# Gated linear attention beside an MLP: the recurrence's running products, block products and carry one round earlier, the split of keys and queries right behind the fourth states, the queries' negation later

## The chip, the core and the metric

The program runs on one core of a Trainium2 chip. The metric is the device time of one execution in microseconds (us). The kernel computes four transformer layers one after the other; the change touches only one function, `gla`, and in it only the written-out order of the work.

## What is computed

Four layers, each an attention-like half and a feed-forward half, over 8 batches of 512 tokens with 128 channels. The change lies where the kernel runs two of these halves together: the feed-forward half of layer 1 (8 experts of 128 by 512) and the attention half of layer 2, a gated linear attention with 8 heads of 32 complex channels:

```python
u = silu(x @ W_in.T + b_in)
q, k, v, a = complex(u @ W_qkva.T + b_qkva)          # (b, 512, 8, 32) each
mag2 = a.real * a.real + a.imag * a.imag
a = a * (rsqrt(mag2) * sigmoid(log(mag2)))           # |a| is the decay, a/|a| a turn of phase
kv = einsum('blhd,blhe->blhde', k, v)
_, h = associative_scan(lambda c1, c2: (c1[0]*c2[0], c2[0]*c1[1] + c2[1]), (a, kv), axis=1)
y = einsum('blhd,blhde->blhe', q, h)
x = x + ga * (silu(y @ W_y.T + b_y) @ W_out.T + b_out)
```

The kernel takes the phases out of the scan: with U the running product of a/|a| along the tokens, q and k are multiplied ("turned") by U or its conjugate, and the scan is left with real decays. It then works by blocks of 32 tokens (and 8 and 16 within them).

## The kernel before

**Stages.** `gla` runs 19 stages, numbered n = 0 to 18. Each of the engines PE (TensorE), DVE (VectorE), ACT (ScalarE) and POOL (GpSimd) walks all stages in its own program, in order, and waits on counting semaphores. A stage mixes work of several batches: `sg` names the group of four heads whose scan is computed (stages 2 to 17), `tg` the group whose q, k and decays are prepared for the next stage (1 to 16), `mg` the group whose projections are made for the stage after that (0 to 15; norm and input projection are made with group 0), `ob` a batch whose output projection is made (even stages from 4 to 18), `half` one half of the experts of a batch (stages 0 to 13). So stages 2 to 13 carry everything; 14 to 17 have no expert matmuls; an even stage from 4 on has the output steps, an odd one has not.

**Order.** Within a stage the order is the tuple `ORDER`, a list of (what, which). Every engine takes from it the steps for which it has a function, so that one list sets the order on all four. A step that an engine's function ignores costs it nothing.

**The steps that matter here.** Four rounds i = 0 to 3 of 128 tokens each: `scores (i, 0..3)` (192 small matmuls, L1279), `gains i` (64 small matmuls, L1295), both on PE; `sums i` and `states i` on DVE (L1530 to L1536; L1545, L1548), which wait for them; `outputs (i, 0..4)` on PE (L1315, L1321), which wait for DVE's sums and states of that round. PE's `scores (i+1, 0)` waits for DVE's `states i`.

Preparation of group `tg`, nearly all on DVE: `decays` (L1580 to L1594), `run0` and `run1` (running products within 16 tokens, 7 and 8 steps of three small operations, L1614 to L1617), `values` (L1601, waits for PE's L1335), `blocks` (products over blocks, L1619 to L1639), `carry` (U, L1645 to L1648, then ACT negates one plane of it, L1492), `turned` (six operations of 128x1024, L1654 to L1657, the first of which waits for ACT's negation), `split` (Q, six operations, L1665; then the keys `ks`, L1667, and queries `qs`, L1669). `split` waits for the last scores of the stage, since these read the old Q and K. POOL's part of `split` (K, six operations, L1245) waits for `kh` of `turned` and for the last scores. ACT's part negates one plane of each Q (L1496); PE's `scores (0, 0)` of the next stage waits for ACT's Q and POOL's K, PE's `keys` (L1260) for DVE's `ks`:

```python
elif i: ...                                             # scores (i, 0) for i > 0 waits for DVE's s and h
else:
    e.wait_ge(act.steps, act.at(was("qneg")))
    e.wait_ge(pool.steps, pool.at(was("K")))
```

`make units` is a chain: DVE (L1566), ACT (L1463 to L1468), POOL (L1229 to L1235, four operations), and DVE's `logs` (L1569). On POOL it stands ahead of `split`.

Output of batch `ob`: `out hidden` (PE, L1373), `out gate` (DVE L1674 and L1676, then three on ACT: L1422, L1424, L1502), `out gated` (DVE, L1679), `out last` (PE L1377, ACT L1505, DVE L1683). PE's `keys` of the next stage waits for ACT's L1505.

**The dense matmuls.** 16 pairs `up i` and `down i - 4` per stage. `up i` (PE, L1388) writes one PSUM bank, and waits until ACT's Relu (L1510) has read `up i - 1` out of it:

```python
if i:
    e.wait_ge(act.steps, act.at(now(f"r{i - 1}")))
e.matmul(P[2], fc[:, n % 2, ts(f, C)], hs[:, n % 2], ...)    # up i
```

ACT follows each Relu by a Square (L1512), for which `down i` (PE, L1402) waits. `up 4 n` also waits for DVE's `root n` (L1689). In an even stage `down 12` to `down 15` are left to the next stage, where they stand as `down -4` to `down -1`; in an odd stage they come at its end. SP loads the experts' weights into two slots each, every load behind the `up` or `down` that used the slot last.

Of the kernel before, what the change touches and what calls it, by code (L numbers as in the profile page):

```python
# [1077 lines left out]
def gla(k, a, gate_rows, h_rows):  # L1078

    nc = k.nc  # L1080
    with ExitStack() as s:
# [44 lines left out]
        def half_of(ap, i, later_half):  # L1126

            if i == 0:
# [10 lines left out]
                 ("scores", (1, 2)), ("outputs", (0, 2)), ("scores", (1, 3)), ("outputs", (0, 3)), ("outputs", (0, 4)), ("turn", "values"), ("gains", 1),  # L1139
                 ("root", 1), ("up", 4), ("down", 0), ("sums", 1), ("states", 1), ("make", "hidden"), ("up", 5), ("down", 1), ("make", "gate"),  # L1140

                 ("scores", (2, 0)), ("outputs", (1, 0)), ("up", 6), ("turn", "run1"), ("scores", (2, 1)), ("outputs", (1, 1)), ("down", 2),
                 ("scores", (2, 2)), ("outputs", (1, 2)), ("make", "gated"), ("scores", (2, 3)), ("outputs", (1, 3)), ("outputs", (1, 4)), ("gains", 2),
                 ("root", 2), ("up", 7), ("down", 3), ("sums", 2), ("states", 2), ("make", "decay"), ("up", 8), ("down", 4), ("turn", "blocks"),

                 ("scores", (3, 0)), ("outputs", (2, 0)), ("make", "query"), ("scores", (3, 1)), ("outputs", (2, 1)), ("scores", (3, 2)),
                 ("outputs", (2, 2)), ("make", "key"), ("scores", (3, 3)), ("outputs", (2, 3)), ("outputs", (2, 4)), ("gains", 3), ("turn", "carry"),
                 ("up", 9), ("down", 5), ("make", "units"), ("sums", 3), ("states", 3), ("root", 3), ("up", 10), ("down", 6), ("turn", "turned"),

                 ("outputs", (3, 0)), ("up", 11), ("outputs", (3, 1)), ("outputs", (3, 2)), ("down", 7), ("outputs", (3, 3)), ("outputs", (3, 4)),  # L1150
                 ("out", "hidden"), ("make", "logs"), ("up", 12), ("down", 8), ("out", "gate"), ("up", 13), ("down", 9), ("turn", "split"), ("up", 14),
                 ("down", 10), ("up", 15), ("down", 11), ("out", "gated"), ("out", "last"), ("down", 12), ("down", 13), ("down", 14), ("down", 15),
                 ("residual", 0))
# [18 lines left out]
        def units():  # L1172
# [17 lines left out]
            with nc.Block() as block:  # L1190
# [217 lines left out]
                def _(e):  # L1408
# [61 lines left out]
                    def turn(what):  # L1470
# [22 lines left out]
                        elif what == "split":  # L1493
# [1098 lines left out]
def build(nc, a, counts, upto=99, first=0):  # L2592
    k = Kernel(nc, counts)
    k.dram = a
    with k.stack:
# [22 lines left out]
        if first <= 3 <= upto:  # L2618
            with ExitStack() as s:
                load(k, a, "gla", s)  # L2620
                gla(k, a, gate_rows, h_rows)
# [123 lines left out]
```

## Time and profile before

| what | value |
|---|---|
| three runs | 4273.81, 4292.37, 4297.87 us; median 4292.37 |
| profiled execution | 4287.15 us, its span 4285.4 us |
| mean granted TensorE clock of that execution | 0.859 of full speed |
| busy share of the span | PE 86%, DVE 54%, ACT 36%, POOL 18% |
| stages 2 to 13 | 947.5 to 2039.3 us, 88 to 96 us each |
| stages 14 to 16 | 2039.3 to 2278.0 us, 82.6, 76.3 and 79.9 us |

The span runs from the first to the last instruction; the profiled execution's own time has 1.75 us more around it. Stages are told apart by PE's `keys` (L1260), which begins each from stage 2 on: 947.5, 1035.6, 1125.0, 1216.9, 1309.0, 1400.6, 1493.4, 1584.3, 1674.6, 1765.6, 1855.3, 1943.2, 2039.3, 2121.8, 2198.2 and 2278.0 us. Stage 7, from 1400.6 to 1493.4 us, is the one that is read closely below.

### The profile page before, as it was taken

To read this page: it belongs to the slowest core of one execution; us is meant where nothing else is said; L and a number is where in the kernel's file an instruction comes from. 1 tells how busy PE (TensorE), PEld (TensorE's weight loads), DVE (VectorE), ACT (ScalarE), POOL (GpSimd) and SP (SyncE) were. 2 spreads that over 40 slices of the span, in tenths; PEclk is the share of its full clock that TensorE was granted. 3 is DMA by queue.
4 is the path that set the end of the run, shared out by engine and by line. 5 is a ranking of instruction groups with operands and counts; after the bars stand their busy time and mean duration, and the time that the engine had idled before them with its cause. 6 is when DMAs were issued, how large, how long until landed. Compare 5 with 4: busy or idle time off the path is not lost. (4 is left out here: it accounts for less than half of the span.)

```text
span 4285.4 us, 124546 instructions
## 1 busy us (share of the span) xinstructions
PE 3686.3 (86%) x55640; PEld 2276.7 (53%) x55640; DVE 2300.0 (54%) x5899; ACT 1558.3 (36%) x2877; POOL 761.2 (18%) x724
## 2 busy tenths in 40 slices
PE   3877776689898888998876987999999999999986
PEld 2336664235554455554554433666666666666672
DVE  3757775267667666676672112444444444444445
ACT  2653333363344443444210433333333333333323
POOL 1212221011112111122110001222222222222210
PEclk9886667798888888988655998999999999999967
DMA  2000000221111111110000000000000000000000
GB/s 83 0 0 1 1 1 1 75 62 37 41 33 41 44 33 39 39 42 27 3 3 17 0 21 40 2 3 2 2 2 2 2 2 3 2 2 2 2 3 22
DMA packets 37030, 79.22 MB, mean 18 GB/s; under 512 B 7568, under 2 KB 11025, under 8 KB 35345
## 3 DMA queue, kind: packets, MB, share of 16 engines
q1 hardware_dynamic: 36496, 71.25, 5.1%
q8 instruction: 440, 7.21, 0.7%
q14 instruction: 94, 0.76, 0.1%
HBM read 66.91 MB, written 4.33 MB: 17 GB/s over the span
## 5 line engine op out<-in xcount | busy, mean ns | idle before, releaser
L2129 PE MATMUL ps<-d_hp,d_w_qk 128*128 128x512 f32 x1024 | 545.8, 629 | 2.7 <-DVE d_hp L2386 2.7
L1388 PE MATMUL ps<-g_hs,g_fc 128*128 128x512 f32 x448 | 289.8, 733 | 82.0 <-ACT g_hidden L1510 75.9
L1510 ACT ACTIVATE g_hidden<-ps 128x512 f32<-128x512 f32 x224 | 133.1, 594 | 377.5 <-PE ps L1388 377.5
L2207 POOL TENSOR_TENSOR d_sq<-d_QK 128x512 f32<-128x512 f32 x128 | 133.0, 1039 | 759.5 <-ACT d_QK L2249 754.1
L1402 PE MATMUL ps<-g_hidden,g_proj 128*128 128x512 f32 x448 | 263.6, 685 | 0.0
L1279 PEld LDWEIGHTS ps<-g_Q,g_K 32*32 32x32 f32 x12288 | 193.9, 113 | 130.1 <-issue 46.6
L1279 PE MATMUL ps<-g_Q,g_K 32*32 32x32 f32 (+1 forms) x12288 | 224.9, 218 | 28.1 <-DVE g_H L1548 12.0
L1229 POOL TENSOR_TENSOR g_tmp<-g_rs 128x512 f32<-128x512 f32 x16 | 26.7, 1667 | 1029.9 <-ACT g_rs L1468 1029.9
L2227 ACT ACTIVATE d_F<-ps 128x128 f32<-128x128 f32 x256 | 70.8, 276 | 381.0 <-PE ps L2043 379.9
L2129 PEld LDWEIGHTS ps<-d_hp,d_w_qk 128*128 128x128 f32 x1024 | 162.5, 190 | 81.9 <-issue 63.4
L1388 PEld LDWEIGHTS ps<-g_hs,g_fc 128*128 128x128 f32 x448 | 82.4, 217 | 191.5 <-ACT g_hidden L1510 144.6
L2185 POOL TENSOR_TENSOR d_M<-d_A,w_joins 128x128 f32<-128x128 f32 (+1 forms) x128 | 114.7, 916 | 385.6 <-ACT d_A L2221 385.6
L2352 DVE TENSOR_TENSOR d_r<-d_r,ps 32x128 f32<-32x128 f32 x192 | 55.0, 286 | 216.5 <-PE ps L2137 121.7
L2086 PEld LDWEIGHTS ps<-d_r,d_Y 32*32 32x32 f32 x2048 | 86.8, 110 | 153.1 <-issue 38.0
L1295 PE MATMUL ps<-g_V,g_KT 32*32 32x64 f32 x4096 | 144.0, 268 | 25.4 <-issue 5.8
L1402 PEld LDWEIGHTS ps<-g_hidden,g_proj 128*128 128x128 f32 x448 | 97.7, 223 | 123.6 <-issue 106.4
L794 PE MATMUL ps<-att_kg,att_qx 32*128 32x96 f32 x1024 | 121.7, 354 | 41.9 <-DVE att_qx L708 27.3
L2036 PE MATMUL ps<-d_QK 128*128 128x128 f32 x1024 | 157.5, 300 | 0.0
L2355 DVE COPY d_W<-ps 32x128 f32<-32x128 f32 x256 | 71.5, 279 | 157.2 <-PE ps L2086 156.1
L2221 ACT ACTIVATE d_A<-d_A 32x128 f32<-32x128 f32 x256 | 78.6, 307 | 210.9 <-DVE d_A L2313 206.3
L2036 PEld LDWEIGHTS ps<-d_QK 128*128 128x128 f32 x1024 | 132.7, 202 | 33.7 <-issue 30.0
L2180 POOL TENSOR_TENSOR d_D<-d_D,w_upto 128x512 f32<-128x512 f32 x64 | 81.0, 1265 | 381.5 <-ACT d_D L2217 381.5
(473 smaller groups left out, 8009.2 us busy)
## 6 DMA issues: line engine op xcount, KB each, us to landing
g_hs<-gate_rows SPq DMA_DIRECT2D x56, 256.0 KB, 3.5
g_fc<-in_c_fc_dram SPq DMA_DIRECT2D x56, 256.0 KB, 3.9
g_proj<-in_c_proj_dram SPq DMA_DIRECT2D x56, 256.0 KB, 2.8
d_QK<-in_conv_qk_dram SPq DMA_DIRECT2D x2, 2048.0 KB, 6.8
X<-in_x_dram SPq DMA_DIRECT2D x1, 2048.0 KB, 11.0
w_c_fc<-in_c_fc_dram SPq DMA_DIRECT2D x1, 2048.0 KB, 7.8
w_c_proj<-in_c_proj_dram SPq DMA_DIRECT2D x1, 2048.0 KB, 12.2
ex_root<-gate_rows SPq DMA_DIRECT2D x1, 2048.0 KB, 15.0
```

The source lines that it names most:

```text
L794: ins = e.matmul(scored[:, g, b], qx[ts(g, 32), q, 4 * u + b, :, :].rearrange("p h q -> p (h q)"), kg[ts(g, 32), q, 4 * u + b, :], start=T ...
L1279: ins = e.matmul(later(scored, n_), keys_, queries(n_, planes, r_, 4 * i + j), start=(turn_ == 0 and part == 0 and n_ != 1), stop=(part == 1),
L1295: ins = e.matmul(P[1][ts(h4, 32), 256 + j * 64:320 + j * 64], KT[rows, (KR, KI)[part], i, ts(h4, 32)], V[rows, i, 4 * c["sg"] + h4, (slice ...
L1388: e.matmul(P[2], fc[:, n % 2, ts(f, C)], hs[:, n % 2], start=True, stop=True).then_inc(pe.steps, pe.did(now(f"u{i}")))
L1402: e.matmul(P[3], proj[:, n % 2, f, :], r[:, (16 * c["half"] + i) % 5], start=(c["half"] == 0 and i == 0), stop=(c["half"] == 1 and i == 15 ...
L1510: e.activation(r[:, slot], P[2], ACT.Relu).then_inc(act.steps, act.did(now(f"r{i}")))
L2036: ins = e.matmul(mk[:, ts(h, C)], QK[:, 1, H, t], QK[:, part - 1, H, t], start=True, stop=True)
L2086: ins = e.matmul(b[rows, 256 + 32 * h:288 + 32 * h], Y[rows, y, h], rv[rows, g, h], start=True, stop=True, tile_position=(32 * j, 32 * j))
L2129: ins = e.matmul(b, w_qk[:, j, c, ts(H, C)], hp_of(u)[:, j:j + T], start=(j == 0), stop=(j == TAPS - 1))
L2180: e.tensor_tensor(D[:, g], D[:, g], k.w["upto3"][:].unsqueeze(1).to_broadcast([C, 4, C]), ALU.mult).then_inc(pool.steps, pool.did(f"d{n}"))
L2185: e.tensor_tensor(M[:, a, levels], A32[:, a].unsqueeze(1).to_broadcast([C, many, 4, 32]), k.w["joins"][:, levels].unsqueeze(2).to_broadcas ...
L2207: e.tensor_tensor(squares(x), qk, qk, ALU.mult).then_inc(pool.steps, pool.did(f"{tag}sq{x}"))
```

## The change

Only `ORDER` and one name change. `run1` moves from round 2 to round 1, ahead of `values`; `blocks` from the end of round 2 to `run1`'s old place; `carry` from round 3 to the end of round 2, between `up 8` and `up 9`; `turned` from behind `states 3` into round 3, ahead of `make units` and `sums 3`; `split` from behind `out gate` and `logs` to right behind `states 3` and `root 3`. ACT's negation of Q, which was ACT's part of `split`, is a step of its own, `negate`, behind `up 14` and `down 10`. `up 9` to `up 12` and `down 5` to `down 8` move forward, `up 9` to `up 11` into rounds 2 and 3; the five `outputs (3, ...)` now stand together; `make logs` moves behind `up 15`.

```diff
-                 ("scores", (1, 2)), ("outputs", (0, 2)), ("scores", (1, 3)), ("outputs", (0, 3)), ("outputs", (0, 4)), ("turn", "values"), ("gains", 1),
-                 ("root", 1), ("up", 4), ("down", 0), ("sums", 1), ("states", 1), ("make", "hidden"), ("up", 5), ("down", 1), ("make", "gate"),
-
-                 ("scores", (2, 0)), ("outputs", (1, 0)), ("up", 6), ("turn", "run1"), ("scores", (2, 1)), ("outputs", (1, 1)), ("down", 2),
+                 ("scores", (1, 2)), ("outputs", (0, 2)), ("scores", (1, 3)), ("outputs", (0, 3)), ("outputs", (0, 4)), ("turn", "run1"), ("turn", "values"),
+                 ("gains", 1), ("root", 1), ("up", 4), ("down", 0), ("sums", 1), ("states", 1), ("make", "hidden"), ("up", 5), ("down", 1), ("make", "gate"),
+
+                 ("scores", (2, 0)), ("outputs", (1, 0)), ("up", 6), ("turn", "blocks"), ("scores", (2, 1)), ("outputs", (1, 1)), ("down", 2),
                  ("scores", (2, 2)), ("outputs", (1, 2)), ("make", "gated"), ("scores", (2, 3)), ("outputs", (1, 3)), ("outputs", (1, 4)), ("gains", 2),
-                 ("root", 2), ("up", 7), ("down", 3), ("sums", 2), ("states", 2), ("make", "decay"), ("up", 8), ("down", 4), ("turn", "blocks"),
-
-                 ("scores", (3, 0)), ("outputs", (2, 0)), ("make", "query"), ("scores", (3, 1)), ("outputs", (2, 1)), ("scores", (3, 2)),
-                 ("outputs", (2, 2)), ("make", "key"), ("scores", (3, 3)), ("outputs", (2, 3)), ("outputs", (2, 4)), ("gains", 3), ("turn", "carry"),
-                 ("up", 9), ("down", 5), ("make", "units"), ("sums", 3), ("states", 3), ("root", 3), ("up", 10), ("down", 6), ("turn", "turned"),
-
-                 ("outputs", (3, 0)), ("up", 11), ("outputs", (3, 1)), ("outputs", (3, 2)), ("down", 7), ("outputs", (3, 3)), ("outputs", (3, 4)),
-                 ("out", "hidden"), ("make", "logs"), ("up", 12), ("down", 8), ("out", "gate"), ("up", 13), ("down", 9), ("turn", "split"), ("up", 14),
-                 ("down", 10), ("up", 15), ("down", 11), ("out", "gated"), ("out", "last"), ("down", 12), ("down", 13), ("down", 14), ("down", 15),
-                 ("residual", 0))
+                 ("root", 2), ("up", 7), ("down", 3), ("sums", 2), ("states", 2), ("make", "decay"), ("up", 8), ("down", 4), ("turn", "carry"), ("up", 9),
+                 ("down", 5),
+
+                 ("scores", (3, 0)), ("outputs", (2, 0)), ("make", "query"), ("scores", (3, 1)), ("outputs", (2, 1)), ("up", 10), ("down", 6),
+                 ("turn", "turned"), ("scores", (3, 2)), ("outputs", (2, 2)), ("make", "key"), ("scores", (3, 3)), ("outputs", (2, 3)), ("outputs", (2, 4)),
+                 ("gains", 3), ("up", 11), ("down", 7), ("make", "units"), ("sums", 3), ("states", 3), ("root", 3), ("turn", "split"), ("up", 12),
+                 ("down", 8), ("outputs", (3, 0)), ("outputs", (3, 1)), ("outputs", (3, 2)), ("outputs", (3, 3)), ("outputs", (3, 4)), ("out", "hidden"),
+                 ("up", 13), ("down", 9), ("out", "gate"), ("up", 14), ("down", 10), ("turn", "negate"), ("up", 15), ("down", 11), ("make", "logs"),
+                 ("out", "gated"), ("out", "last"), ("down", 12), ("down", 13), ("down", 14), ("down", 15), ("residual", 0))
@@ ACT's turn(what)
-                        elif what == "split":
+                        elif what == "negate":
                             for i in range(3):
```

## Rows read from the trace of the kernel before

**Rows 1.** The page's busy time: engine, us, share of the span, instructions
```profile
PE 3686.3 (86%) x55640; PEld 2276.7 (53%) x55640; DVE 2300.0 (54%) x5899; ACT 1558.3 (36%) x2877; POOL 761.2 (18%) x724
```
**Rows 2.** Busy time by stretch: us, PE, PEld, DVE, ACT, POOL, granted clock, DMA share, GB/s
```profile
947.50:2039.30 1091.80, 982.27 (x19624) 556.19 (x19623) 747.19 (x1976) 451.05 (x788) 181.86 (x126) 0.86 0.12 37
2039.30:2278.00 238.70, 180.65 (x4707) 131.34 (x4705) 165.99 (x480) 48.60 (x89) 28.20 (x27) 0.60 0.01 3
...
1400.60:1493.40 92.80, 84.78 (x1637) 47.09 (x1637) 60.20 (x161) 35.84 (x63) 14.91 (x10) 0.83 0.15 45
```
**Rows 3.** PE's waits in stages 2 to 13: total us, times, longest
```profile
PE ps L1388 <- ACT g_hidden L1510: 60.9, 27, 6.7
```
**Rows 4.** Timeline of PE, stage 7: start, us, work, idle before it and releaser
```profile
1462.05 2.19 PE L1295 MATMUL ps<-g_V,g_KT 32*32 32x64 f32 x64
1464.17 2.08 PE L1388 MATMUL ps<-g_hs,g_fc 128*128 128x512 f32 x2
...
1485.61 2.08 PE L1388 MATMUL ps<-g_hs,g_fc 128*128 128x512 f32 x2 [4.24 <-ACT g_hidden L1510]
1487.48 6.08 PE L1402 MATMUL ps<-g_hidden,g_proj 128*128 128x512 f32 x10
1493.40 1.04 PE L1260 MATMUL ps<-w_ident,g_m_ks 128*128 128x128 f32 x8
```
**Rows 5.** Timeline of ACT, stage 7
```profile
1452.48 0.61 ACT L1510 ACTIVATE g_hidden<-ps 128x512 f32<-128x512 f32 x1
...
1484.66 0.42 ACT L1496 ACTIVATE g_Q<-g_Q 128x256 f32<-128x256 f32 x1 [1.32 <-DVE g_Q L1665]
1484.98 0.58 ACT L1510 ACTIVATE g_hidden<-ps 128x512 f32<-128x512 f32 x1
```
**Rows 6.** Timeline of DVE, stage 7
```profile
1424.54 0.69 DVE L1601 TENSOR_TENSOR g_V<-ps,w_b_v 128x512 f32<-128x512 f32 x1 [8.41 <-PE ps L1335]
...
1460.59 0.42 DVE L1530 TENSOR_TENSOR g_S<-ps,w_gla_mask 128x256 f32<-128x256 f32 x1 [4.10 <-PE ps L1279]
...
1464.38 0.29 DVE L1536 TENSOR_TENSOR g_S<-g_S,ps 128x128 f32<-128x128 f32 x1 [2.84 <-PE ps L1295]
...
1466.79 1.22 DVE L1654 TENSOR_TENSOR g_m_qs<-g_raw_qka,g_U 128x1024 f32<-128x1024 f32 x1
...
1472.30 2.28 DVE L1655 TENSOR_TENSOR g_m_ks<-g_raw_qka,g_U 128x1024 f32<-128x1024 f32 x1
...
1477.73 6.89 DVE L1665 TENSOR_TENSOR g_Q<-g_unit_qh,g_F 128x512 f32<-128x512 f32 x6
```
**Rows 7.** Timeline of POOL, stage 7
```profile
1469.18 2.12 POOL L1229 TENSOR_TENSOR g_tmp<-g_rs 128x512 f32<-128x512 f32 x1 [74.22 <-ACT g_rs L1468]
...
1477.23 7.11 POOL L1245 TENSOR_TENSOR g_K<-g_kh,g_E 128x512 f32<-128x512 f32 x6
```
**Rows 8.** Timeline of PE: ends of stages 9 and 8, of stage 1
```profile
1667.19 2.08 PE L1388 MATMUL ps<-g_hs,g_fc 128*128 128x512 f32 x2 [6.72 <-ACT g_hidden L1510]
...
1574.70 1.13 PE L1388 MATMUL ps<-g_hs,g_fc 128*128 128x512 f32 x2 [1.25 <-ACT g_hidden L1510]
...
1578.91 1.53 PE L1388 MATMUL ps<-g_hs,g_fc 128*128 128x512 f32 x2 [2.23 <-ACT g_hidden L1510]
...
940.00 2.07 PE L1388 MATMUL ps<-g_hs,g_fc 128*128 128x512 f32 x2 [8.67 <-ACT g_hidden L1510]
```
**Rows 9.** Timeline of PE, DVE and POOL at the ends of stages 14 to 16
```profile
2118.90 2.07 PE L1377 MATMUL ps<-g_xb,w_W_out 128*128 128x512 f32 x2 [8.32 <-DVE g_xb L1679]
...
2182.32 2.86 PE L1315 MATMUL ps<-g_S,g_V 32*64 32x32 f32 x64 [3.64 <-DVE g_H L1548]
...
2198.17 1.97 PE L1260 MATMUL ps<-w_ident,g_m_ks 128*128 128x128 f32 x8 [10.97 <-DVE g_m_ks L1667]
...
2275.10 2.07 PE L1377 MATMUL ps<-g_xb,w_W_out 128*128 128x512 f32 x2 [7.75 <-DVE g_xb L1679]
...
2182.12 1.22 DVE L1654 TENSOR_TENSOR g_m_qs<-g_raw_qka,g_U 128x1024 f32<-128x1024 f32 x1
...
2189.47 7.16 POOL L1245 TENSOR_TENSOR g_K<-g_kh,g_E 128x512 f32<-128x512 f32 x6 [7.70 <-DVE g_kh L1657]
```

## The prediction

> **What bounds the kernel now.** The page first: PE is busy 86% of the span, DVE 54% [rows 1]. By stretches, stages 2 to 13 hold 982 us of PE work in 1091.8, stages 14 to 16 181 us in 238.7 at a mean clock of 0.60 [rows 2]. So PE is the bound of the first stretch, and what can be won there is PE's idle time, or PE time at the lower clock. PE's waits come next: 60.9 us in 27 waits of `up` (L1388) for ACT's Relu are by far the largest entry [rows 3]. They lie like this: seven long ones of 4.24 to 6.72 us near the end of stages 2, 3, 5, 7, 9, 11, 13 (36.3 us together; the shortest in [rows 4], the longest in [rows 8]); two in each of the even stages 4 to 12, 1.01 to 2.23 us (15.6 us; stage 8's in [rows 8]); and 9.0 us in ten places that the change leaves alone (six of 1.26, four of 0.35 us). Stage 1 has one more, of 8.67 us [rows 8].
>
> Then three timelines of stage 7. ACT's Relu of `up 14` starts at 1484.98, right behind the last negation of Q, which had waited for DVE's Q [rows 5]; `up 15`, which needs the bank that this Relu reads, starts at 1485.61 [rows 4]. DVE makes the six Q from 1477.73 to 1484.6, since `turned`, begun at 1466.79, comes only behind `states 3` and lasts 11 us [rows 6]. So the gap is DVE's lateness passed on by ACT, which stands in its queue before the negation while a Relu that PE wants waits behind it. DVE itself is not full: it sits 8.41 us before `values`, 4.10 before `sums 3`, 2.84 inside it [rows 6].
>
> **The change, part by part, in stage 7.** *`run1` ahead of `values`.* Eight steps at about 0.76 us (1430.5 to 1436.6 before) are 6.0 us, into an idle 8.41 [rows 6]: nothing. In the even stages that idle is shorter by `normed`; `values` comes some 0.5 us late there at most, behind which PE has `gains 1`, `up 4`, `down 0`. Nothing. *`blocks`* (5.2 us) takes the place of the longer `run1`: nothing. *`carry`* (3.6 us) right behind `states 2`: U is ready at about 1450.6. ACT meets its negation behind the Relu of `up 8`, which it does at 1452.48 [rows 5], so ACT does not wait; that needs 2 us of slack and has them. *`turned`* then runs from about 1454.4 (ACT's negation done) with POOL idle, six operations of 1.22 us (the first of them in [rows 6]), 7.4 us, to 1461.8, and `units` 0.7 behind it. Now it stands ahead of `sums 3`. DVE before waited for these until 1460.59 and 1464.38 [rows 6]; with two pairs of `up` and `down` (some 3.8 us) put ahead of them on PE they come at about 1464.5 and 1468.3. Slack 2 us for the first, 5.8 for the one that counts. Nothing, and the rival of the other sign below.
>
> *`root 3` and `up 12`.* `up 12` now follows `down 7`, two pairs earlier in effect. DVE needs `sums`' last step, `states 3` and `root 3`, 2.7 us, from the end of `gains 3`; PE has `up 11` and `down 7` for that, 1.9 us at full clock, 3.8 at half, and behind gains they ran at half (2.08 for two records, 1.0 to 1.1 elsewhere) [rows 4]. A wait of 0 to 1.5 us per stage; I take 0.5, 6 us over twelve.
>
> *`split`* starts at about 1471 instead of 1477.7, but with PE's work ahead of it moved 4 us later this is more than 10 us earlier against PE. Q is done by 1478. `negate` comes on ACT behind `up 14`, about 1482. ACT no longer waits there; its 1.5 us of negations stand ahead of the Relu of `up 15`, for which only `down 15` asks, behind four other `down`. So the long gaps go: -36.3. In even stages DVE's `out gate` now stands behind `split`, which is over by then, and ACT's three operations for it (1.9 us) stand before the Relu of `up 14`; I leave 1.0 of each stage's two gaps: -15.6 + 5 = -10.6.
>
> *POOL.* Its chain starts when ACT has made `units`, behind `up 11` now, behind `up 9` before. Measured from the end of `gains 3` that is the same place. It takes 8 us for units and 7.11 for K [rows 7]: from 1473 to about 1488. PE then wants K for `scores (0, 0)`, one `keys` after its own end: before at 1494.4, now near 1490 or less. Slack 1 to 2 us where there were 10. Nothing, but thin. The Trainium skill, GPSIMD Engine Reference, section Specifications, says that GpSimd shares its SBUF interfaces with VectorE and contends with VectorE instructions that have two SBUF inputs. The trace agrees: `turned` takes 1.22 us an operation without POOL and up to 2.28 beside it [rows 6]. By that rule the new neighbour of `units` (Q instead of `turned`) has two inputs as well, so the price in stages 2 to 13 stays; in stages 14 and 15 it is new (below).
>
> *Stage 1.* It has no recurrence on PE, so DVE is later against PE: `run1` delays `values` and `root 1` by 1.8 us and `turned` before `root 3` delays `up 12` by some 1.3. The 8.67 us gap goes, then PE waits for POOL's K. Bounds 2 and 8.7; I take -5.
>
> *Stages 14 to 16.* No pairs here, DVE close behind PE. Stage 15: DVE had `turned` from 2182.12, POOL K 7.16 us from 2189.47, PE's `keys` only at 2198.17 after 10.97 us [rows 9]. Now `turned` is over by 2175.5, `split` starts at the end of `states 3`, about 2182; POOL beside it lengthens Q to 6.9, `ks` is ready near 2190, K near 2191. PE's `keys` at about 2189.7: -8.5. Stages 14 and 16 end with `out last` waiting for `gated` behind `split` (8.32 and 7.75 us) [rows 9]. Now `gated` waits only for PE's own `out hidden`, `out gate` and ACT: 4.4 us. -3.9 and -3.3. The 3.64 us before `outputs (3, 0)` [rows 9] may lose up to 1.5 if POOL no longer runs beside `states 3`; taken as 0. Together -15.7.
>
> *Clock.* Behind each of eight long gaps the matmuls run at the lower of the two levels: `up 15` took 2.08 us for two records, and `down 11` to `down 15` 6.08 for ten [rows 4], where 12 records at the full rate of 0.43 take 5.2. Over the eight stages 7.0 to 8.1 us (3.2 against 1.9 in the even one) make 19 us. With the gap gone these should go too. Against that: the five `outputs (3, ...)` now stand together, 3 us of small matmuls with no dense one between, and behind such stretches (`scores`, `outputs`, `gains`) PE also fell to the lower level [rows 4]. One such fall per stage would cost 1.7 us, 20 in all. The bounds of this item are -19 and +20; I take -10, half of the gain, since 3 us is shorter than the 4.5 us ahead of 1464. The Trainium skill, TensorE: Matmul & The Clock Gate, section on HAM oscillation, has the rule that idle gaps between bursts throw the clock back to half and that the burst behind pays. The trace agrees behind the gaps. By the rule alone, without the new block, the sum would be 9 us lower.
>
> **SP.** The loads wait for the same `up` and `down`, which come earlier; DMA is busy 12% [rows 2]. Nothing.
>
> **Sum.** -36.3 - 10.6 + 6 - 5 - 15.7 - 10 = -71.6 us. From the profiled execution, 4287.15, that is 4215.5. The median of the three runs is 5.2 above it, and the runs spread over 24 us; I put 2.5 on: 4218.
>
> **The rivals.** (a) *POOL becomes the bound of stages 2 to 13.* K comes at 1488 to 1490, PE asks at 1488 to 1490. For: slack falls from 10 us to under 2, and every us that PE wins is one that POOL does not. Against: in odd stages DVE is through with Q, `ks` and `qs` before K ends, so K should rather be shorter than 7.11 us. If K is 2 us late per stage, 24 us come back: 4242. (b) *The clock takes the gain.* `outputs (3)` in one block costs a fall in every stage and the ends gain nothing: +20 instead of -10, 4248. For: half-speed matmuls behind every small stretch; against: dense pairs now also split `scores (3, ...)`. (c) *`turned` holds up the recurrence: slower.* It stands ahead of `sums 3` in DVE's queue. If it starts late, because ACT reaches U's negation late or runs it behind the evacuations of `query`, then `sums 3`, `states 3`, `root 3` and with them `up 12` and `outputs (3, 0)` wait. It decides once the delay is over the 5.8 us of slack. If all of `turned` fell behind `gains 3`, 7.4 us per stage, 89 us over twelve stand against 72 won: 4304. Against it: ACT gets there at 1453.7 with the operand ready. (d) *Nothing that can be measured.* ACT still waits, for Q at `negate`, or the waits reappear at `up 10` to `up 12`: 4280. That would need Q 4 us later than worked out.
>
> **Chances.** Forecast 0.60, (a) 0.14, (b) 0.13, (c) 0.06, (d) 0.07. What a measurement can tell from no change is about 0.5%, 21 us. (a) and (b) are still faster; so faster 0.87, same 0.07, slower 0.06. Range: below, the full 19 us of clock, no wait at `up 12` and all of stage 1 give about 4188; above, (a) and (b) with a little of both, 4258.
>
> **What would show it.** After: the wait of L1388 for ACT in stages 2 to 13 falls from 60.9 us to 14 to 22, no single one over 2; L1496 no longer ends its idle with DVE's Q; DVE's `turned` operations all at 1.22 us and before `sums 3`; PE waits for L1679 and L1667 at the ends of stages 14 to 16 nearly gone; POOL's K ends within 3 us of `scores (0, 0)`; the mean clock of stages 2 to 13 at 0.86 to 0.88. A stage of 88 us or more, a wait of L1279 for g_K, or a wait of L1388 for g_hs over 1.5 us would make it wrong.

## The result, and the profile after

| | us |
|---|---|
| changed kernel | 4236.88, median of 4 runs (4232.26 to 4240.60) |
| kernel before, beside it | 4295.12, median of 4 (4273.81 to 4309.92) |
| ratio, with its 95% interval | 0.9868 (0.9824 to 0.9911) |
| the changed kernel again, two more times | 4241.44 (5 runs), ratio 0.9886 (0.9866 to 0.9907); 4246.05 (4 runs), 0.9897 (0.9869 to 0.9926) |
| profiled execution | 4237.54, its span 4235.8, mean clock 0.862; before 4287.15, 4285.4, 0.859 |

The change makes the kernel faster by 1.0 to 1.3%, some 50 us (43 to 58 by the medians) where the sum had 72. The measured 4236.88 lies 19 us above the forecast of 4218, inside its range of 4188 to 4258. The profiled executions are 49.6 us apart. From the stage borders of the two traces: up to the keys of stage 2 -3.6 us, stages 2 to 13 -32.4 (1091.8 to 1059.4), stages 14 to 16 -12.5, all that follows -1.1. In stages 2 to 13 PE's idle time fell by 25.8 us (109.5 to 83.7) and its busy time by 6.6.

The page's busy line, and the two stretches that answer to [rows 1] and [rows 2] (us, then PE, PEld, DVE, ACT, POOL, granted clock, DMA share, GB/s):

```profile
PE 3676.4 (87%) x55640; PEld 2273.3 (54%) x55640; DVE 2277.5 (54%) x5899; ACT 1556.2 (37%) x2877; POOL 728.4 (17%) x724
```
```profile
943.90:2003.30 1059.40, 975.69 (x19623) 554.84 (x19622) 721.35 (x1978) 448.26 (x788) 153.53 (x129) 0.87 0.12 38
2003.30:2229.60 226.30, 178.68 (x4708) 130.14 (x4706) 171.11 (x480) 48.52 (x89) 28.48 (x27) 0.60 0.01 3
```

PE's waits in stages 2 to 13 of the changed kernel (us in total, times, longest). Line numbers from `ORDER` on are one lower than before, so L1387 is [rows 3]'s L1388:

```profile
PE ps L1387 <- ACT g_hidden L1509: 19.3, 23, 2.8
PE ps L1320 <- issue: 12.1, 10, 2.6
PE ps L1278 <- issue: 10.2, 12, 2.2
PE ps L1387 <- DVE g_hs L1688: 5.4, 7, 0.8
PE ps L1294 <- issue: 4.4, 8, 0.9
...
PE ps L1278 <- POOL g_K L1244: 2.2, 2, 1.8
```

The entry of 60.9 us is down to 19.3, inside the 14 to 22 of the forecast, though its longest is 2.8 where none was to be over 2. Three others have come or grown: `up 12` waits for DVE's `root 3` (L1688), `scores (0, 0)` for POOL's K (L1244), and the three "issue" entries, in which PE waited for nothing that the profile shows, are 26.7 us where the same view of the kernel before had 10.0, 5.8 and 5.8, or 21.6. In two more traces of the changed kernel the three are 25.6 and 29.2.

Now stage 7 (keys 1385.1 to 1468.0, 82.9 us for 92.8), as four timelines: start, us, work, idle before it and what ended it. PE:

```profile
1454.10 1.12 PE L1387 MATMUL ps<-g_hs,g_fc 128*128 128x512 f32 x2 [0.77 <-DVE g_hs L1688]
...
1462.79 1.12 PE L1387 MATMUL ps<-g_hs,g_fc 128*128 128x512 f32 x2
1463.75 4.45 PE L1401 MATMUL ps<-g_hidden,g_proj 128*128 128x512 f32 x10
...
1469.01 1.21 PE L1278 MATMUL ps<-g_Q,g_K 32*32 32x64 f32 x62
```

`up 15` (1462.79) has no wait ahead of it, and the ten records behind it take 4.45 us where [rows 4] has 6.08: the gap of 4.24 us and the slow matmuls behind it have both gone. ACT and DVE:

```profile
1463.30 1.23 ACT L1495 ACTIVATE g_Q<-g_Q 128x512 f32<-128x512 f32 x3
1464.43 0.57 ACT L1509 ACTIVATE g_hidden<-ps 128x512 f32<-128x512 f32 x1
```
```profile
1437.46 1.23 DVE L1653 TENSOR_TENSOR g_m_qs<-g_raw_qka,g_U 128x1024 f32<-128x1024 f32 x1 [3.75 <-ACT g_U L1491]
...
1447.99 0.42 DVE L1529 TENSOR_TENSOR g_S<-ps,w_gla_mask 128x256 f32<-128x256 f32 x1 [2.53 <-PE ps L1278]
...
1453.36 0.68 DVE L1688 TENSOR_TENSOR g_hs<-g_hx,g_hs 128x512 f32<-128x512 f32 x1
1453.96 4.96 DVE L1664 TENSOR_TENSOR g_Q<-g_unit_qh,g_F 128x512 f32<-128x512 f32 x6
1458.84 3.43 DVE L1666 TENSOR_TENSOR g_m_ks<-g_kh,g_E_lg 128x512 f32<-128x512 f32 x2
```

ACT's three negations run in one piece of 1.23 us, without a wait, behind the Relu and Square of `up 14`. On DVE `turned` begins at 1437.46; between its end and the first `sums 3` the engine still idles for 2.53 us, so it holds nobody up. Q is done 4.4 us before ACT turns to it. POOL:

```profile
1455.40 1.08 POOL L1228 TENSOR_TENSOR g_tmp<-g_rs 128x512 f32<-128x512 f32 x1 [76.02 <-ACT g_rs L1467]
...
1460.00 7.49 POOL L1244 TENSOR_TENSOR g_K<-g_kh,g_E 128x512 f32<-128x512 f32 x6
```

K ends at 1467.49, 1.5 us before `scores (0, 0)` at 1469.01: as thin as forecast, and enough except at the start of stages 2 and 3 (the 2.2 us above). From there on K has 0.6 to 3.4 us to spare at the end of an odd stage, and 3.2 to 8.3 at the end of an even one.

That is not how every stage runs. In stages 2 to 9 of this trace POOL's first operation starts 1.4 us behind DVE's Q, and the two engines' work is as shown. In stages 10 to 13 it starts 1.9 to 2.4 us behind it, and then it is POOL that is held, here in stage 13:

```profile
1985.86 2.63 DVE L1664 TENSOR_TENSOR g_Q<-g_unit_qh,g_F 128x512 f32<-128x512 f32 x6
```
```profile
1988.25 4.14 POOL L1228 TENSOR_TENSOR g_tmp<-g_rs 128x512 f32<-128x512 f32 x1 [80.44 <-ACT g_rs L1467]
```

DVE's whole `split` takes 5.0 us in those four stages, and 11.1 in the other eight.

The even stages kept their length (542.1 us in the six of them for 541.5), the odd ones fell from 550.3 to 517.3. In the even ones PE's waits for ACT's Relu did fall, from 29.0 us to 17.1, but its other idle time rose by some 8 us and its busy time by 4.6, with 146.8 us at the lower clock for 138.8. (Two more traces of the changed kernel have even stages of 545.1 and 546.1 us, with 160.4 and 153.6 us at the lower clock. There is one trace of the kernel before.) One of the waits that are left is at the end of stage 8, DVE first, then PE:

```profile
1542.74 4.95 DVE L1664 TENSOR_TENSOR g_Q<-g_unit_qh,g_F 128x512 f32<-128x512 f32 x6
1547.62 3.42 DVE L1666 TENSOR_TENSOR g_m_ks<-g_kh,g_E_lg 128x512 f32<-128x512 f32 x2
...
1553.78 0.74 DVE L1673 TENSOR_SCALAR g_xb<-ps,w_b_y 128x512 f32<-128x512 f32 x1
```
```profile
1557.93 1.13 PE L1387 MATMUL ps<-g_hs,g_fc 128*128 128x512 f32 x2 [2.76 <-ACT g_hidden L1509]
```

PE's `out hidden` ended at about 1551.6. `out gate` (L1673) reads it only at 1553.78, since `split` stands ahead of it and takes 11.1 us. ACT's three operations for the gate follow that, and the Relu that `up 15` needs follows them: 2.76 us of idle PE. It is the longest such wait. In the other two traces stage 8 has 1.05 and 1.06 us there; `out hidden` ran at the lower clock in these and took 5.40 us instead of 3.70, so the gate was hardly late.

Last, PE at the end of stage 1 and of stages 14 to 16, against [rows 8] and [rows 9]:

```profile
896.78 2.03 PE L1387 MATMUL ps<-g_hs,g_fc 128*128 128x512 f32 x2 [5.34 <-ACT g_F L1484]
```
```profile
2067.50 2.86 PE L1314 MATMUL ps<-g_S,g_V 32*64 32x32 f32 x64 [4.83 <-DVE g_H L1547]
...
2082.77 2.08 PE L1376 MATMUL ps<-g_xb,w_W_out 128*128 128x512 f32 x2 [4.02 <-DVE g_xb L1678]
...
2153.22 1.97 PE L1259 MATMUL ps<-w_ident,g_m_ks 128*128 128x128 f32 x8 [4.14 <-DVE g_m_ks L1666]
...
2226.64 2.08 PE L1376 MATMUL ps<-g_xb,w_W_out 128*128 128x512 f32 x2 [4.01 <-DVE g_xb L1678]
```

The waits for L1679 fell from 8.32 and 7.75 to about 4, the one for the keys of stage 16 from 10.97 to 4.14. Against that `outputs (3, 0)` of stage 14 waits 4.83 us for the states, where it had been 3.64, as in stage 15. The states ran beside POOL's `units` before too; now they also meet the start of its K, and their four 128x32 operations take 3.42 us for 2.22.

### The profile page after: what moved, and what is told of

It reads as the page before. It is cut to its first block and busy times, and to the rows that moved or that the text cites. A ratio compares the mean times of both kernels' runs of the same rounds, so it can differ in the third digit from the quotient of the medians.

```text
span 4235.8 us, 124560 instructions
## 1 busy us (share of the span) xinstructions
PE 3676.4 (87%) x55640; PEld 2273.3 (54%) x55640; DVE 2277.5 (54%) x5899; ACT 1556.2 (37%) x2877; POOL 728.4 (17%) x724
## 5 line engine op out<-in xcount | busy, mean ns | idle before, releaser
L2128 PE MATMUL ps<-d_hp,d_w_qk 128*128 128x512 f32 x1024 | 545.9, 629 | 2.7 <-DVE d_hp L2385 2.7
L1387 PE MATMUL ps<-g_hs,g_fc 128*128 128x512 f32 x448 | 287.6, 728 | 42.2 <-ACT g_hidden L1509 24.2
L1401 PE MATMUL ps<-g_hidden,g_proj 128*128 128x512 f32 x448 | 254.7, 664 | 0.0
L1387 PEld LDWEIGHTS ps<-g_hs,g_fc 128*128 128x128 f32 x448 | 82.9, 216 | 154.3 <-ACT g_hidden L1509 82.0
L2216 ACT ACTIVATE d_D<-d_D 128x512 f32<-128x512 f32 x64 | 40.3, 629 | 294.8 <-DVE d_D L2299 294.8
## 6 DMA issues: line engine op xcount, KB each, us to landing
w_c_proj<-in_c_proj_dram SPq DMA_DIRECT2D x1, 2048.0 KB, 12.5
```

The costliest lines, as they stand in the source:

```text
L1387: e.matmul(P[2], fc[:, n % 2, ts(f, C)], hs[:, n % 2], start=True, stop=True).then_inc(pe.steps, pe.did(now(f"u{i}")))
L1401: e.matmul(P[3], proj[:, n % 2, f, :], r[:, (16 * c["half"] + i) % 5], start=(c["half"] == 0 and i == 0), stop=(c["half"] == 1 and i == 15 ...
L2128: ins = e.matmul(b, w_qk[:, j, c, ts(H, C)], hp_of(u)[:, j:j + T], start=(j == 0), stop=(j == TAPS - 1))
```

## Experiments

Each was timed beside the kernel before; ratios are to that, with the 95% interval. "Idle" is PE's idle time in stages 2 to 13, "low" the time of that stretch in which the granted clock stood at the lower level (before: 109.5 and 303.8 us; changed kernel, three traces: 83.7, 81.0, 84.6 and 279.9, 307.2, 279.9).

**The changed kernel again**, to have its spread beside the variants.

> The changed kernel itself once more, on the chip on which the three below run, so that they can be held against it. Both theories: 0.985 to 0.990 of the kernel before, about 4237 us.

> The changed kernel again, as the one that the three below are held against: ratio 0.985 to 0.991.

4241.44 and 4246.05 us (ratios in the first table). The forecast's shape stands, its size doesn't.

**1. ACT's negation alone.** The kernel before, with only this:

```diff
-                 ("down", 10), ("up", 15), ("down", 11), ...
+                 ("down", 10), ("turn", "negate"), ("up", 15), ("down", 11), ...
@@ ACT's turn(what)
-                        elif what == "split":
+                        elif what == "negate":
```

> The kernel before with one edit: ACT's three negations of Q are a step of their own behind `up 14` and `down 10`, nothing moves on DVE, POOL or PE. Theory A (ACT's place in its queue made the gaps; DVE's lateness by itself costs nothing in stages 2 to 13): the Relu of `up 14` no longer stands behind the negations, so the seven gaps of 4.24 to 6.72 us and the one of 8.67 go, L1388's waits for ACT fall from 60.9 to 15 to 25 us, with some of the clock 40 to 50 us in all, 4245 to 4255 us, ratio 0.988 to 0.991; stages 14 to 16 stay at 82.5, 76.4 and 79.8 us. Theory B (Q must come earlier, the moves on DVE carry the gain): Q is as late as before, the negations now hold the Relu of `up 15`, `down 15` and the end of the stage wait instead; 4285 to 4295 us, ratio 0.998 to 1.000.

4253.14 us (4 runs), 0.9906 (0.9891 to 0.9921): some 40 us, most of what the whole change brings. Idle 83.0, the same as with the whole change. Stages 14 to 16 took 236.8 for 238.7. What is left of the late Q, in the waits of PE and at the end of stage 7 on ACT and PE:

```profile
PE ps L1402 <- ACT g_hidden L1512: 8.1, 6, 3.0
```
```profile
1474.22 0.42 ACT L1496 ACTIVATE g_Q<-g_Q 128x256 f32<-128x256 f32 x1 [1.32 <-DVE g_Q L1665]
1474.55 0.58 ACT L1510 ACTIVATE g_hidden<-ps 128x512 f32<-128x512 f32 x1
```
```profile
1475.84 1.12 PE L1402 MATMUL ps<-g_hidden,g_proj 128*128 128x512 f32 x2 [2.06 <-ACT g_hidden L1512]
```

ACT waits for Q as before, but the Relu behind its wait is that of `up 15`, for which only `down 15`, the last of the stage, asks.

**2. The negation early, behind the early `split`.** The changed kernel, with

```diff
-("root", 3), ("turn", "split"), ("up", 12),
+("root", 3), ("turn", "split"), ("turn", "negate"), ("up", 12),
...
-("down", 10), ("turn", "negate"), ("up", 15),
+("down", 10), ("up", 15),
```

> The changed kernel with ACT's negations put back to where `split` now stands, behind `root 3` and ahead of `up 12`; DVE, POOL and PE keep their order. Theory A (the place of the negations in ACT's queue decides): ACT waits there for the third Q, some 5 us from the end of `root 3`, with the Relu and Square of `up 12` behind it, so `down 8` comes 4 to 5 us late in each of stages 2 to 13, with a fall of the clock behind it; 50 to 65 us lost against the changed kernel, 4285 to 4305 us. Theory B (the earlier Q is what counts): 4237 to 4245 us.

4247.28 us (6), 0.9902 (0.9876 to 0.9929), idle 83.9: no loss, and the expectation of 50 to 65 us lost was wrong. ACT, then PE, in stage 7:

```profile
1471.71 0.42 ACT L1495 ACTIVATE g_Q<-g_Q 128x256 f32<-128x256 f32 x1 [1.74 <-DVE g_Q L1664]
1472.03 0.58 ACT L1509 ACTIVATE g_hidden<-ps 128x512 f32<-128x512 f32 x1
```
```profile
1468.77 2.00 PE L1314 MATMUL ps<-g_S,g_V 32*64 32x32 f32 x64
...
1472.66 2.07 PE L1387 MATMUL ps<-g_hs,g_fc 128*128 128x512 f32 x2 [0.68 <-ACT g_hidden L1509]
```

ACT does wait for Q and holds the Relu of `up 12` back, but PE has the block of `outputs (3, ...)` to do meanwhile, and only 0.68 us show. Together with run 1: an early Q and a late negation are two cures for one gap, either of which takes nearly all of it. The early negation was run only with PE's new order, in which the block of outputs stands behind the Relu that ACT holds back; whether it would do as well without that block was not run.

**3. PE's new order without DVE's.** The changed kernel with DVE's and ACT's preparation at its old places (`run1`, `blocks`, `carry`, `turned`, `split`), `negate` and PE's pairs and outputs at the new ones.

```diff
-("outputs", (0, 4)), ("turn", "run1"), ("turn", "values"),
+("outputs", (0, 4)), ("turn", "values"),
...
-("root", 3), ("turn", "split"), ("up", 12),
+("root", 3), ("turn", "turned"), ("up", 12),
...
-("out", "gate"), ("up", 14),
+("out", "gate"), ("turn", "split"), ("up", 14),
```

> The changed kernel with DVE's and ACT's preparation steps in their old places between the new places of PE's work: `run1` behind `up 6`, `blocks` ahead of round 3, `carry` behind `gains 3`, `turned` behind `root 3`, `split` behind `out gate`; the pairs and the negation as in the changed kernel. Theory A (with the pairs moved forward DVE has to come forward too, or Q, K and ks end behind PE): `turned` begins at the end of round 3, Q is ready 10 us later against PE than in the changed kernel, the last Relu and POOL's K are waited for, 4 to 6 us per stage; 4285 to 4310 us. Theory B (the gain lies in where the dense pairs stand, through the clock): within 10 us of the changed kernel, 4237 to 4247 us.

4325.20 us (5), 1.0081 (1.0067 to 1.0095): slower than the kernel before by 35 us and slower than expected. Idle 115.7, low 398.7. PE's waits:

```profile
PE ps L1376 <- DVE g_xb L1678: 21.7, 5, 4.9
PE ps L1401 <- ACT g_hidden L1511: 21.4, 6, 4.3
```

The pairs moved forward leave fewer behind DVE's late preparation to cover it. Set against run 1, whose preparation is as late, the new place of the pairs and outputs costs 72 us.

**4. DVE's new order without PE's.** Run 1 with DVE's preparation at the new places; pairs and `outputs (3, ...)` stay where the kernel before has them.

```diff
-("turn", "values"), ("gains", 1),
+("turn", "run1"), ("turn", "values"), ("gains", 1),
...
-("outputs", (2, 1)), ("scores", (3, 2)),
+("outputs", (2, 1)), ("turn", "turned"), ("scores", (3, 2)),
...
-("root", 3), ("up", 10), ("down", 6), ("turn", "turned"),
+("root", 3), ("turn", "split"), ("up", 10), ("down", 6),
...
-("turn", "split"), ("up", 14),
+("up", 14),
```

> The fourth corner: the pairs of `up` and `down` and the `outputs (3, ...)` where the kernel before has them, DVE's preparation steps (`run1`, `blocks`, `carry`, `turned`, `split`) in their new places, the negation behind `up 14`. Theory A (the moves on DVE only pay for the pairs having been moved forward, and at the ends of stages 14 to 16; where the pairs stand is worth nothing): PE's idle time in stages 2 to 13 as in the run that moved the negation alone (83 us) or a little less, stages 14 to 16 at 224 to 228 us, 4235 to 4247 us, ratio 0.987 to 0.990. Theory B (the new places of the pairs carry part of the gain): 10 us or more slower than the changed kernel, ratio 0.991 to 0.995.

**4224.02 us (5), 0.9832 (0.9812 to 0.9852)**: the fastest kernel of this study, ahead of both. Neither theory had it: the new place of the pairs and outputs is neither worth nothing nor worth something, it costs. The three medians of the changed kernel are 13, 17 and 22 us above this one, though none was taken beside it; beside it ran the kernel of run 5, 17 us slower. The interval lies clear of those of the changed kernel's two repeats and overlaps that of its first measurement. The outputs went back with the pairs here; run 6 takes them by themselves. Stages 2 to 13, and PE's waits in them:

```profile
942.90:1988.10 1045.20, 982.34 (x19623) 560.24 (x19622) 671.51 (x1976) 448.61 (x788) 155.50 (x126) 0.86 0.13 39
```
```profile
PE ps L1388 <- ACT g_hidden L1510: 14.2, 12, 2.6
PE ps L1321 <- issue: 9.6, 9, 2.3
PE ps L1279 <- issue: 8.4, 8, 2.1
...
PE ps L1295 <- issue: 2.7, 8, 0.5
...
PE ps L1388 <- DVE g_hs L1689: 0.2, 1, 0.2
```

Idle is 62.9, 20.8 less than with the whole change: 5.2 at L1689 (`up 12` no longer stands one pair behind `gains 3`), 6.0 in the issue entries, 5.1 at L1510, 2.2 at K, whose entry is gone, and the rest in smaller ones. POOL and DVE in stage 7:

```profile
1443.56 4.14 POOL L1229 TENSOR_TENSOR g_tmp<-g_rs 128x512 f32<-128x512 f32 x1 [73.08 <-ACT g_rs L1468]
...
1451.06 5.23 POOL L1245 TENSOR_TENSOR g_K<-g_kh,g_E 128x512 f32<-128x512 f32 x6
```
```profile
1441.16 2.63 DVE L1665 TENSOR_TENSOR g_Q<-g_unit_qh,g_F 128x512 f32<-128x512 f32 x6
```

Here, and in eleven of this run's twelve stages, POOL's first operation starts when DVE's Q is nearly over and is held (4.14 us) while `ks` and `qs` run; Q takes 2.63 instead of 4.96, and K then runs alone in 5.23: it ends 5.5 us before `scores (0, 0)` at 1461.79, not 1.5.

**5. `out gate` ahead of keys and queries.** The changed kernel, with `ks` and `qs` taken out of `split` into a step `held`:

```diff
-("out", "gate"), ("up", 14),
+("out", "gate"), ("turn", "held"), ("up", 14),
@@ DVE's split, between Q and ks
+                        elif what == "held":
```

> The changed kernel with DVE's four operations for `ks` and `qs` taken out of `split` and put behind `out gate`. Theory A (the even stages won nothing because `ks` and `qs`, slowed from 2.6 to 6.3 us beside POOL's K, hold up `out gate`, and ACT's part of it the Relu of `up 14`): `out gate` starts when `out hidden` is done, 2 us earlier, the gap of 2.76 us in stage 8 falls to about 1, stages 4, 6, 8, 10, 12 get 1 to 2 us shorter, 5 to 10 us in all, 4228 to 4232 us. Theory B (the even stages' time went to the clock): the gap moves, the time of the even stages does not change by more than 0.5 us each; 4235 to 4239 us.

> The kernel with `ks` and `qs` behind `out gate` once more, as the one that the three beside it are held against: ratio 0.985 to 0.989 of the kernel before.

4228.63 us (5), 0.9868 (0.9847 to 0.9889), and again 4241.09 (6), 0.9868 (0.9835 to 0.9902), beside 0.9886 and 0.9897 of the changed kernel. On the first occasion the changed kernel itself, run beside it, was 13 us slower (4241.44), but the intervals overlap, and the second median is as high as the changed kernel's. The time alone doesn't tell. The trace, end of stage 8, DVE and PE:

```profile
1555.76 0.75 DVE L1674 TENSOR_SCALAR g_xb<-ps,w_b_y 128x512 f32<-128x512 f32 x1 [5.68 <-PE ps L1372]
...
1556.88 1.28 DVE L1667 TENSOR_TENSOR g_m_ks<-g_kh,g_E_lg 128x512 f32<-128x512 f32 x2
```
```profile
1560.26 1.13 PE L1387 MATMUL ps<-g_hs,g_fc 128*128 128x512 f32 x2 [1.01 <-ACT g_hidden L1509]
```

`out gate` now waits for PE, the gap is 1.01 us, and `ks` takes 1.28 us where it had 3.42 beside POOL's K. All ten such gaps in this kernel's two traces are 1.01; the fifteen in the changed kernel's three are 1.00 to 2.76, and what they have over 1.01 comes to 2.7, 1.5 and 0.6 us a trace. So the late gate is real and small. Idle is 80.1 and 85.5, and the even stages take 543.4 and 545.9 us, as in the changed kernel: the theory that the gate had kept them long, 5 to 10 us, did not hold.

**6. The block of outputs spread.** The changed kernel with `outputs (3, ...)` between `up 12` and `down 9` instead of in one block:

```diff
-("down", 8), ("outputs", (3, 0)), ..., ("outputs", (3, 4)), ("out", "hidden"), ("up", 13), ("down", 9),
+("outputs", (3, 0)), ("down", 8), ("outputs", (3, 1)), ("outputs", (3, 2)), ("up", 13), ("outputs", (3, 3)), ("outputs", (3, 4)), ("down", 9), ("out", "hidden"),
```

> The changed kernel with the five `outputs (3, ...)` spread between `up 12`, `down 8`, `up 13` and `down 9` again, nothing else moved. Theory A (their standing together costs nothing that can be measured): within 5 us of the changed kernel, time at the lower clock in stages 2 to 13 within 10 us of it. Theory B (rival (b) of the prediction, at half strength: the block lowers the clock behind it in some stages, so the gain from the clock was halved): 8 to 15 us faster than the changed kernel, time at the lower clock 15 to 30 us less.

4237.64 us (6), 0.9880 (0.9853 to 0.9906). The changed kernel beside it had 4246.05, 8 us more, with overlapping intervals. Low is 269.7 us, 10 below the least of the changed kernel's three traces, and idle 90.7, some 7 more: only one pair is left between `out hidden` and `up 15`, and PE's gaps behind it in the even stages are 2.2 to 2.8 us, all five. Run 9 spreads the outputs in the same way on top of run 5 and gains nothing. Rival (b), 30 us off the forecast, is out at its size; a cost of the block of some 10 us could hide behind the longer gaps and is not excluded.

**7. Relu of `up 14` ahead of the gate, `root 1` ahead of `run1`.** On top of run 5:

```diff
-("turn", "run1"), ("turn", "values"), ("gains", 1), ("root", 1),
+("root", 1), ("turn", "run1"), ("turn", "values"), ("gains", 1),
...
-("out", "gate"), ("turn", "held"), ("up", 14), ("down", 10), ("turn", "negate"),
+("up", 14), ("down", 10), ("out", "gate"), ("turn", "held"), ("turn", "negate"),
```

> The changed kernel with three moves of single steps: `ks` and `qs` behind `out gate` on DVE (as in the run before, which gave 0.9868 against 0.9886 of the changed kernel), `out gate` with ACT's three operations behind `up 14` and `down 10`, and `root 1` ahead of `run1`. Theory A: the gap of 1.01 us before `up 15` in each of the five even stages goes, and the 5.3 us wait of `up 4` in stage 1 falls to 1 or less; 8 to 12 us together and 12 to 18 with the first move, 4220 to 4228 us, ratio 0.983 to 0.986. Theory B (the waits only move to `out last`, which needs ACT's gate, and to the next root): within 4 us of the run before, ratio 0.986 to 0.988.

4235.07 us (4), 0.9867 (0.9839 to 0.9895): no gain over run 5. The 1.01 us before `up 15` has gone and `out last` waits instead:

```profile
PE ps L1376 <- DVE g_xb L1679: 6.2, 5, 1.2
```

The gate is a chain through PE, DVE, ACT, DVE and PE; whichever is put first, some 1.2 us of it show. The 5.34 us of stage 1 stayed too, so `root 1` is not its cause; run 8 shows what is.

**8. `make units` ahead of `turned`.** On top of run 5, with `root 1` first:

```diff
-                 ("turn", "turned"), ("scores", (3, 2)), ...
+                 ("make", "units"), ("turn", "turned"), ("scores", (3, 2)), ...
-                 ("gains", 3), ("up", 11), ("down", 7), ("make", "units"), ("sums", 3),
+                 ("gains", 3), ("up", 11), ("down", 7), ("sums", 3),
```

> The kernel with `ks` and `qs` behind `out gate`, and `make units` moved from behind `up 11` to ahead of `turned`, `root 1` ahead of `run1`. Theory A (the chain of units, moved back with `up 11`, costs: `up 0` of stage 1 waits 5.34 us instead of 1.67, `outputs (3, 0)` of stages 14 and 15 waits up to 4.8 us beside POOL's units, `scores (0, 0)` of stage 2 waits 1.8 us for K): these three waits fall to 2, 2.5 and 0 us, 6 to 9 us in all, against some us lost where POOL now runs beside `turned` (1.2 to 2.2 us an operation) with slack ahead of `sums 3`; 4220 to 4228 us, ratio 0.983 to 0.987. Theory B (`turned`, slowed, ends behind `gains 3` and `sums 3`, `states 3`, `up 12` wait): 5 us or more slower than the kernel beside it.

4274.85 us (8), 0.9960 (0.9940 to 0.9981): 34 us lost against run 5's second measurement. Idle 105.0. PE's waits, and DVE in stage 7:

```profile
PE ps L1387 <- DVE g_hs L1689: 32.0, 12, 3.3
```
```profile
1461.92 0.74 DVE L1547 TENSOR_SCALAR g_H<-g_H 128x32 f32<-128x32 f32 x1
...
1464.62 1.28 DVE L1689 TENSOR_TENSOR g_hs<-g_hx,g_hs 128x512 f32<-128x512 f32 x1
```

POOL now runs beside the states and `root 3`: the operations of 128x32 take 0.74 and 0.46 us where they took 0.18, `root 3` 1.28 where it took 0.68, and `up 12` stands right behind them. That is rival (c)'s place, DVE late for the recurrence in front of `up 12`, reached by another way.

The same run shows what held stage 1 up. With POOL's `units` of stage 0 started at 881.26 us instead of 885.38, DVE's decays and ACT's part of them come earlier, and the 5.34 us before `up 0` are 2.31, with `root 0` as the last to come:

```profile
892.66 1.85 PE L1387 MATMUL ps<-g_hs,g_fc 128*128 128x512 f32 x2 [2.31 <-DVE g_hs L1689]
```

Run 4, with `units` behind `up 9` as before, has 1.66 there.

**9. Runs 5, 6 and `root 1` first together.**

> The kernel with `ks` and `qs` behind `out gate`, with the `outputs (3, ...)` spread as in the run before and `root 1` ahead of `run1`. Theory A (the block of outputs costs nothing): within 4 us of the kernel beside it. Theory B (spreading them saves half-speed time, as its 270 against 280 to 307 us in stages 2 to 13 may say): 6 to 12 us faster, 4216 to 4222 us, ratio 0.983 to 0.985.

4239.14 us (4), 0.9864 (0.9841 to 0.9888), low 303.8, idle 89.1: nothing beyond run 5, which had 4241.09 beside it.

## Why the prediction was right and wrong

The direction, the place and the mechanism of the gain were right; the size was 22 us off against the profiled execution (-71.6 forecast, -49.6 measured), of which stages 2 to 13 hold 18.5. The measured 4236.88 lies closer to the 4242 of rival (a) and the 4248 of (b) than to 4218, but nothing shows that K or the block of outputs made the difference. The items that the sum had priced miss by some 10 us together; the other 12 belong to what the sum had at nothing.

**Long gaps, -36.3: right.** All seven are gone. Run 1 adds what the prediction did not see: it credited an early Q and a late negation together, and the late negation alone would have done nearly all of it, in one line.

**Even stages, -10.6: -7.9.** The gaps are 1.90, 1.01, 2.76, 1.01 and 1.01; in the two repeats the item comes to -9.0 and -10.0. The step that failed is "DVE's `out gate` now stands behind `split`, which is over by then": in most stages `split` takes 11.1 us, because POOL's K falls on `ks` and `qs` (3.4 and 2.9 us for 1.28 each). Run 5 shows it, at 0.6 to 2.7 us. The stages themselves won nothing (542.1 us for 541.5): other waits and time at the lower clock took the gain back.

**`up 12`, +6: right.** 5.4 us in seven waits of 0.77. `root 3` is the last of DVE's work there as worked out.

**"Two pairs put ahead", cost nothing: wrong.** This is the largest error, 13 to 22 us by run 4, of which the 5.4 at `up 12` had been priced. How much of it belongs to the block of outputs, which moved with the pairs, stays open: run 6 leaves room for some 10 us. The prediction took the pairs' place as cover for DVE and asked only whether DVE would be late. It never priced what those pairs had covered at the end of the stage and around `gains 3`: `up 9` waits 0.43 us for a Relu behind ACT's evacuations in some eleven stages, the issue entries grow by 5.1 us, `up 12` waits for `root 3`, and POOL has 1.5 us left instead of 5.5. The issue entries are not the pairs' alone: they are 20.7 in run 4 and 25.6 to 29.2 in the changed kernel's three traces, but 18.5 in run 3, which has the pairs at the new place and DVE's steps at the old. They grow with both together; what they consist of, the traces don't say.

**POOL: right, with its thinness.** In stage 7 units took 4.6 us, not 8, K 7.5; rival (a) priced 2 us of wait per stage, and it came in two stages only. The Trainium skill, GPSIMD Engine Reference, section Specifications, has GpSimd contend with VectorE instructions that run in a 2-port perf mode or have two SBUF inputs; the traces agree on `ks` (3.42 against 1.28 us). The 128x32 operation of run 8 has one tensor input and is slowed too (0.74 against 0.18); no run here shows in which mode it ran. The prediction took the price of the new neighbour to be the old one; in four of twelve stages it fell on POOL instead.

**Stage 1, -5: -3.6.** The 8.67 is gone, but 5.34 us stand before `root 0`'s pair where 1.67 stood, and 2.97 at 910.50 where 1.38 stood. The 5.34 wait for ACT's decays, which follow POOL's units of stage 0, and these are made behind `up 11` instead of `up 9`. Run 7 excludes `root 1`, and runs 4 and 8, with earlier units, have 1.66 and 2.31 us there. For `units` behind `up 11` the prediction had looked only at K.

**Stages 14 to 16, -15.7: -12.5.** Stage 15 -8.8 (forecast -8.5), 16 -3.5 (-3.3): the sums are right, in part by luck. The wait for the keys of stage 16 fell by 6.8, not 8.5, and 2.3 of stage 15's gain is PE's busy time; in stage 16 the wait for `gated` fell by 3.7 and that for the states grew by 1.3. Stage 14 gave -0.2 for -3.9: the wait for `gated` fell by 4.3, but `outputs (3, 0)` waits 1.19 more, `out hidden` 1.59 it didn't before (`values` behind `run1`), and the rest, 1.3, is in smaller ones. "The 3.64 may lose up to 1.5" had the wrong sign.

**Clock, -10: -6.6 in this pair of traces.** The gain came where the gaps had been: the odd stages have 133.1 us at the lower level for 165.0. The even ones have 8 us more, and a loss at the new block of rival (b)'s size did not come (run 6). One pair of traces settles it badly, since the changed kernel alone spreads over 27 us at the lower level. Over all runs of both kernels the mean granted clock rose from 0.857 to between 0.860 and 0.862, which is some 49 us less at the lower of the two levels, 1.2 GHz; a microsecond there does half the work of one above, so that is worth up to some 25 us of PE's work in the whole program. The traces have less: PE is busy for 3686.3 us in the whole of the one before, and for 3676.4, 3683.6 and 3678.9 in the three of the changed kernel. How much of it is cause, and how much only less idle time, stays open.

**Rivals.** (b) is excluded at its size, (a) is its edge only, (d) did not come. (c) did not come either, since DVE idles 2.5 us between `turned` and `sums 3`; run 8 shows that its mechanism is real, at 34 us for lateness of up to 3.3 us a stage.

**The prediction's own signs.** DVE's `turned` came as said (72 operations of 1.22 to 1.23 us, all before `sums 3`), L1496's wait for Q has gone, and the mean clock of stages 2 to 13 is 0.87. But two of the three signs that were to make it wrong are there: five stages of 88 us or more (91.6 to 95.2; stages 4, 6, 8, 10 and 13), and two waits of `scores (0, 0)` for K. And the waits at the ends of stages 14 to 16 were to be nearly gone, and are 4.0 to 4.1 us each. The signs were set for a sum of -72; they tell rightly that some of its terms failed, though the time fell into the range.

## What to carry to other kernels

When an engine's in-order queue waits for a late operand, ask what is queued behind the wait and who needs that, before making the operand early: moving the waiting instruction one step behind the work that another engine needs gave some 40 of these 50 us. Work moved forward to cover one engine is taken from where it covered another; price both ends, and try the reorder of the feeding engines without that of the bound one. Two engines that slow each other should overlap where neither result is next on the path: the overlap of POOL and DVE cost nothing that showed beside Q, up to 1.8 us in an even stage beside `ks` and `qs`, and 34 us in all beside the states. And before a single gap is explained, look for it in a second trace of the same kernel: the 2.76 us of stage 8 were 1.05 and 1.06 in the others.

## What the runs showed of the hardware

- Beside POOL, DVE's operations grow by factors that depend on what meets what: Q (six operations) took 2.63 us alone and 4.96 beside `units`; `ks` (two) 1.28 and 3.43 beside K; the 128x32 operation with a single tensor input 0.18 and, in stage 7 of run 8, up to 0.74.
- The price can fall on either side, and a microsecond's difference in when POOL starts goes with which. In the 48 stages of run 4 and of the changed kernel's three traces, wherever POOL's first `units` operation started up to 1.8 us behind the start of DVE's Q, it took 1.0 to 1.3 us and Q 4.5 to 5.0; wherever it started 1.9 us behind or later, it took 3.5 to 4.4 us and Q 2.6. With DVE idle beside it, in run 8, it took 1.04 us.
- The same kernel spent 279.9, 307.2 and 279.9 us of stages 2 to 13 at the lower clock level in three executions; differences of a single stage between two traces are mostly this, and only sums over stages, or waits, were read as effects.
